# Eight PSUM banks split anew in a four-layer attention and FFN kernel: three banks for scores, three for maxima and small products

## The reference

```
x = x + xattn0(layernorm(x), ctx);  x = x + ffn0(layernorm(x))     # 16 heads of 8, memory slots; GELU
x = x + xattn1(layernorm(x), ctx);  x = x + moe1(layernorm(x))     # q, k RMS-normed; 4 experts, top 2
x = x + xattn2(layernorm(x), ctx);  x = x + moe2(layernorm(x))     # rotary q, k; 8 experts, top 2, and a shared one
x = x + xattn3(layernorm(x), ctx);  x = x + moe3(layernorm(x))     # one head of 128
# x: (4, 512, 128), ctx: (4, 154, 128), all fp32
# xattn: softmax(q k^T / sqrt(d)) v, then an output projection (not in xattn3)
```

## Time and profile before

| | |
|---|---|
| median of 3 runs | 975.82 us (975.11 to 977.1) |
| the profiled execution's own time | 974.97 us |
| its span, first to last instruction | 973.1 us |
| PE busy | 895.2 us (92%) |
| DVE busy | 574.7 us (59%) |
| ACT busy | 443.9 us (46%) |
| attention items of layer 0 | about 45 to 232 us of the span |
| attention items of layer 1 | about 232 to 360 us |
| attention items of layer 2 | about 540 to 655 us |

### The profile page before, as it was taken

How to read it: one execution, slowest core, us unless ns; L and a number is a source line. 1 busy time by engine, 2 the same in 40 slices (tenths; PEclk the granted TensorE clock), 3 DMA queues, 4 the chain that set the end, 5 groups by cost and what they waited for, 6 DMA issues and landing times. The chain is left out here.

```text
span 973.1 us, 15438 instructions
## 1 busy us (share of the span) xinstructions
PE 895.2 (92%) x5522; PEld 638.0 (66%) x5522; DVE 574.7 (59%) x1401; ACT 443.9 (46%) x799; POOL 275.9 (28%) x402
## 2 busy tenths in 40 slices
PE   3799999999998998999989899998999999999776
PEld 3555464646554547888867554547888888788664
DVE  2866758574867556446556477756354454444477
ACT  7365565648575463334322565564233232222330
POOL 6322418183755341012011245331001010010243
PEclk9999999999999999999999999999999999999996
DMA  6000000001022010000000311010000000000001
GB/s 158 6 1 15 3 15 1 15 2 37 3 54 80 2 36 24 1 1 1 2 1 2 87 37 41 29 31 7 1 1 1 2 1 1 1 1 1 2 0 44
DMA packets 27573, 18.10 MB, mean 19 GB/s; under 512 B 6221, under 2 KB 25770, under 8 KB 27370
## 3 DMA queue, kind: packets, MB, share of 16 engines
q1 hardware_dynamic: 27498, 17.12, 6.3%
HBM read 15.63 MB, written 1.05 MB: 17 GB/s over the span
## 5 line engine op out<-in xcount | busy, mean ns | idle before, releaser
L1331 DVE TENSOR_REDUCE mneg<-PS 128x2 f32<-128x308 f32 (+1 forms) x384 | 179.7, 514 | 108.5 <-PE PS L880 107.5
L1494 DVE TENSOR_TENSOR work<-PS,work 128x512 f32<-128x512 f32 (+2 forms) x168 | 114.8, 685 | 169.3 <-PE PS L1065 126.0
L1798 ACT ACTIVATE work<-PS 128x512 f32<-128x512 f32 (+2 forms) x168 | 99.8, 596 | 245.8 <-PE PS L1065 232.0
L1775 ACT ACTIVATE work<-PS 124x512 f32<-124x512 f32 (+1 forms) x272 | 156.3, 599 | 87.6 <-PE PS L1000 86.6
L1079 PEld LDWEIGHTS PS<-down_w,work 128*128 128x128 f32 (+2 forms) x1344 | 157.8, 191 | 5.7 <-DVE work L1494 1.3
L1079 PE MATMUL PS<-down_w,work 128*128 128x128 f32 (+2 forms) x1344 | 158.3, 275 | 1.0 <-DVE work L1494 1.0
L1063 PE MATMUL PS<-xh_sb,arena 128*128 128x512 f32 (+2 forms) x336 | 138.0, 411 | 9.6 <-DVE work L1494 9.6
L1065 PE MATMUL PS<-xh_sb,arena 128*128 128x512 f32 (+2 forms) x336 | 132.7, 395 | 0.0
L1064 PE MATMUL PS<-xl_sb,arena 128*128 128x512 f32 (+2 forms) x336 | 132.1, 393 | 0.0
L1878 POOL TENSOR_SCALAR rstd<-bn_mv 128x4 f32<-128x4 f32 x32 | 7.6, 237 | 436.7 <-DVE bn_mv L1229 436.7
L880 PEld LDWEIGHTS PS<-kb_sb,qxt_sb 97*128 97x128 f32 x256 | 44.2, 191 | 61.7 <-DVE mneg L1331 28.7
(11 more groups left out here) (183 smaller groups left out, 1254.5 us busy)
## 6 DMA issues: line engine op xcount, KB each, us to landing
ctx_rep<-in_ctxT SPq DMA_DIRECT2D x12, 308.0 KB, 3.3
stage<-in_w SPq DMA_DIRECT2D x8, 256.0 KB, 4.0
stage<-in_wg SPq DMA_DIRECT2D x8, 176.0 KB, 2.3
stage<-in_wu SPq DMA_DIRECT2D x8, 176.0 KB, 2.3
x_res<-in_x SPq DMA_DIRECT2D x4, 256.0 KB, 4.0
down_w<-in_w SPq DMA_DIRECT2D x1, 1024.0 KB
down_w<-in_wd SPq DMA_DIRECT2D x8, 128.0 KB
out<-x_res SPq DMA_DIRECT2D x4, 256.0 KB, 2.3
```

The source lines that it names most:

```text
L1331: dve.tensor_reduce(mneg[:, a % 2, t, h0:h0 + 2], PS[:, bank_of["mx", a, m], 0:2 * (KT0 if layer == 0 else KC)].rearrange("p (h n) -> p h ...
L1494: dve.tensor_tensor(HH[0:rows, e % 2, j, :], PS[0:rows, 2 * (n % 2) + 1, :], SS[0:rows, n % 2, :], ALU.mult).then_inc(*sig["h"].mark((i, n)))
L1775: act.activation(p_tile(i, n)[0:rows, :], PS[0:rows, n % 2, :], ACT.Exp, scale=SCALE).then_inc(*sig["p"].mark((i, n)))
L1798: act.activation(SS[0:rows, n % 2, :], PS[0:rows, bank, :], ACT.Silu).then_inc(*sig["act"].mark((i, n)))
```

## The change

During attention items, scores go to banks 0, 1 and 2 in turn (n % 3), and the shared pool is (3, 4, 5). The pair of `k_transposes` may start at any bank, so it is (3, 4) or (4, 5). The bank that `down0` holds may not be 4, so that a pair is left beside it. Nothing else is changed: the same instructions run in the same order on each engine.

```diff
-            return (2, 3, 4, 5) if ITEMS[i_main][0] == "A" else (4, 5)
+            return (3, 4, 5) if ITEMS[i_main][0] == "A" else (4, 5)
...
-                firsts = [n for n in pool if n % 2 == 0 and n + 1 in pool]
+                firsts = [n for n in pool if n + 1 in pool]
...
-                bank = min(pool, key=lambda n: taken_at.get(n, -1))
+                bank = min([n for n in pool if label[0] != "y0" or n != 4], key=lambda n: taken_at.get(n, -1))
...
-                    if n % 2 in taken:
-                        pe.wait_ge(*taken[n % 2])
-                    pe.matmul(PS[0:rows, n % 2, :], KB(layer)[0:K_ALL, a % 2, g, c * rows:(c + 1) * rows],
+                    if n % 3 in taken:
+                        pe.wait_ge(*taken[n % 3])
+                    pe.matmul(PS[0:rows, n % 3, :], KB(layer)[0:K_ALL, a % 2, g, c * rows:(c + 1) * rows],
                               QXT[0:K_ALL, a % 2, g, :], start=True, stop=True).then_inc(*sig["st"].mark((i, n)))
-                    taken[n % 2] = sig["p"].at((i, n))
+                    taken[n % 3] = sig["p"].at((i, n))
...
-                act.activation(p_tile(i, n)[0:rows, :], PS[0:rows, n % 2, :], ACT.Exp, scale=SCALE).then_inc(*sig["p"].mark((i, n)))
+                act.activation(p_tile(i, n)[0:rows, :], PS[0:rows, n % 3, :], ACT.Exp, scale=SCALE).then_inc(*sig["p"].mark((i, n)))
```

## The result

| | before | after |
|---|---|---|
| median | 975.6 us (975.11 to 977.1, 4 runs) | 1002.99 us (1000.96 to 1007.27, 4 runs) |
| ratio to before, 95% interval | | 1.0284 (1.0248 to 1.032) |
| profiled execution, its span, granted clock | 974.97 us, 973.1, 0.975 | 1000.96 us, 999.1, 0.973 |

What follows compares the result with a forecast made beforehand. TensorE, busy 92% of the span and full in mid-item, was taken to bound the kernel. The terms 12 + 8 + 6 + 7 - 3 - 1 = +29 us gave 1005 us, 3% slower, range 987 to 1022.

Steps and rivals of the forecast that it cites:

- What bounds the kernel: TensorE, busy 92% of the span and full in mid-item, so every wait added to its list lengthens the kernel.
- (a): Regular cycle of layers 1 and 2: fourth maximum waits for its own cycle's first reduction; 40 x 0.30 = 12.0 us.
- (b): Attention item starts: transposed queries, with fewer banks, wait for ACT's copies of the keys; 8 us, bounds 4 and 14.
- (c): Where DVE is behind, with normalisation steps ahead of maxima, banks come free late; 13 places, 6 us, bounds 2 and 12.
- (d): Single pieces (attention output, transposed queries, a few by `up0`) get their banks late; 7 us, bounds 3 and 10.
- Given back by scores: Outside the item starts, scores wait less for exponentials thanks to the third score bank; 3 us won back.
- R1: Rival: faster, as 9 to 13 us of score waits go and maxima lose nothing; about 965 us, chance 0.05.
- nearly gone: Sign in the profile after: scores waiting for exponentials would be nearly gone from the list of waits.
- The turn of banks at the end: A3 items: banks 4 and 5 shift by one, so one transpose of x waits instead of three; 1 us won.
- R3: Rival: waits build on each other, upper bounds hold and PE's clock falls more often; 1026 to 1030 us, chance 0.10.

Runs made afterwards that it cites:

- late slots only: Kernel before, with scores in three banks and the shared pool of three only from slot 7 of an attention item on: 993.26 us, ratio 1.0183.
- start-only run: Kernel before, with scores in three banks and the shared pool of three only in slots 0 to 6 of an attention item: 994.92 us, ratio 1.0199.

## Why the prediction was right

- What bounds the kernel: right. Nothing hid the added waits. Layer by layer the loss was forecast as 8, 12 and 8 us and is 8.6, 11.6 and 8. These three add up to 28 and the forecast's terms for the same layers to 30, so 2 us of its sum stand in no stretch; the trace has 28.2.
- (a) The cycle: right. The fourth maximum waits for the first reduction of its own cycle; 2.24 us became 2.54, where 2.5 was forecast, in the changed kernel and in the one with late slots only, and it shrank with the reduction. 40 x 0.30 = 12 us; the waits for DVE rose in 38 places.
- (b) The starts: the mechanism is right, to the forecast 2.6 us at a = 5 (2.62) and the wait that only moves at a = 9. Start and single pieces, less what scores gain there, were put at +9 in the start-only run and came to 9.6 by span x clock, but to 19.4 in time, so that forecast of 985 us was missed by 10. The prediction's own terms had 12 there.
- (c) and (d) were not measured each by itself. The late slots, (a), (c) and a little of (d), were put at 18 and cost 0.0183 of the time, 17.9 us, of which 16.6 in span x clock.
- Given back by scores: 3 us forecast; 4.2 by the ratios, with intervals that overlap, and of these by the table 3.6 of clock and 0.7 of span x clock. What the rival R1 expected of it, 9 to 13, it isn't. The waits of scores are not "nearly gone" either: 12.0 us are left at the weight loads.
- The turn of banks at the end: 1 us forecast, 2 in the trace, 1.7 in the run that has it alone. As forecast, one of the three transposes still waits, 1.4 us in place of 5.6.
- The term that was left out: the clock. I had it in R3 only, as something on top. The changed kernel has 2.6 to 3.5 us more that were not granted. The measured 27 us are by that rough split about 24 of waits and 3 of clock, so the waits alone were put 5 us too high (29), and the missing term made up for more than half of it. That is the part of the hit that was luck. Where the 5 us stand, by span x clock: the late slots had 18 and came to 16.6, the start and the single pieces less the scores' gain had 12 and came to 9.6, and the end, put at 1, gave back 2.2. Each of these differences is within a few times the scatter of its runs, so none is firm by itself.

## What to carry to other kernels

When a ring of buffers loses one, list for each user what now frees its buffer, and set that time against the user's start in the trace. On an in-order engine that is full, each difference that repeats goes straight into the time (0.30 us x 40 here), and it can be checked by shortening the reader.

A wait that is seen at one place says what is late, not what a buffer there would win: ask which wait comes next for the same late engine. Here it was the same ACT copies, two instructions on.

Banks that one piece of code hands out in turn can meet a bank that another piece uses by a fixed number. Taking that bank out of the turn was worth more than any split of the rest.

## What the runs showed of the hardware that was not expected

The granted clock differs between runs of one kernel, and often explains their scatter. The changed kernel took 1000.96 us at 0.973 of full speed granted and 1007.27 at 0.966; the late-slots kernel 991.64 at 0.975 and 998.64 at 0.967, and its four times scatter by 3.1 us but only by 0.5 in span x clock. It isn't all: in the 23 runs of before the times scatter by 1.3 us and span x clock by 1.6. A mean under 1 says that the lower of the two levels (1.2 GHz) was granted for part of the time. Stretches of the changed kernel, the up-projections of layer 2, where PE is full, and the end, where it is busy for 51 of 71 us:

```profile
682.40:928.00 245.60, 239.11 (x1462) 203.85 (x1459) 120.82 (x301) 73.73 (x119) 13.70 (x16) 1.00 0.01 2
928.00:999.10 71.10, 51.08 (x300) 41.88 (x298) 46.16 (x167) 20.17 (x54) 25.62 (x28) 0.86 0.05 16
```

Two parts that sum to 0.9989 and their whole at 0.9961 differed by their clocks alone as far as the split tells. So a change of 0.3% can be told wrongly here without the clock of each run beside it.
